# Two cross attentions in one kernel: where the weights of later stages are split into halves

## The reference

```
# layer 0: 8 heads of 16, no norm
Q = x @ W_q;  K, V = ctx @ W_k, ctx @ W_v
X = x + softmax(Q K^T / sqrt(16)) V @ W_o
x = X + relu(X @ w1.T + b1) @ w2.T + b2          # w1, w2: 512 x 512
# layer 1: 16 heads of 32, layernorm on both inputs
q = layernorm(x) @ Wq.T;  k, v = layernorm(ctx) @ Wkv.T
x = x + softmax(q k^T / sqrt(32)) v @ Wo.T + bo
out = x + silu(x @ W1.T + b1) @ W2.T + b2        # W1: 2048 x 512, W2: 512 x 2048
```

## Time and profile before

| | us |
|---|---|
| median of 3 runs | 5425.91 |
| lowest, highest | 5416.05, 5426.97 |
| the profiled execution | 5431.3 |
| its span on the core | 5429.5 |
| mean granted clock of TensorE | 0.975 of full speed |

### The profile page before, as it was taken

The page is one execution under the profiler, slowest core; times in us unless marked ns, Lnnn a source line. Parts: engine busy times, 40 slices in busy tenths (PEclk is TensorE's granted clock), DMA queues, the critical chain, the costliest instruction groups (busy, mean ns, idle before and its releaser), DMA issues. The chain is left out here.

```text
span 5429.5 us, 93007 instructions
## 1 busy us (share of the span) xinstructions
PE 5216.4 (96%) x27916; PEld 3335.3 (61%) x27916; DVE 4277.0 (79%) x6970; ACT 3251.5 (60%) x5920; POOL 2485.7 (46%) x1165
## 2 busy tenths in 40 slices
PE   8989999999799799999999999999999995999999
PEld 6844444444377566666666666666666662788887
DVE  6689999999577799999999999999999995432331
ACT  4258888888533377777777777777777773322222
POOL 0000000000000299999999999999999995000000
PEclk9989999999799799999999999999999997999999
DMA  7521111111344311111111111111111112332320
GB/s 218 130 51 36 38 39 39 38 37 32 93 124 128 107 33 45 46 45 46 37 41 45 46 45 45 32 46 45 46 45 33 45 33 86 117 97 87 100 93 24
DMA packets 340342, 341.18 MB, mean 63 GB/s; under 512 B 188304, under 2 KB 196368, under 8 KB 337936
## 3 DMA queue, kind: packets, MB, share of 16 engines
q1 hardware_dynamic: 339984, 336.71, 23.5%
HBM read 227.57 MB, written 108.92 MB: 62 GB/s over the span
## 5 line engine op out<-in xcount | busy, mean ns | idle before, releaser
L465 DVE TENSOR_REDUCE a_maxes<-a_mscore 128x1 f32<-128x458 f32 (+4 forms) x5376 | 3044.8, 626 | 218.6 <-PE a_mscore L526 163.1
L441 ACT ACTIVATE a_prob<-a_score 128x512 f32<-128x512 f32 x4992 | 2635.6, 602 | 891.8 <-PE a_score L535 855.9
L535 PE MATMUL a_score<-a_q,a_k 97*128 97x512 f32 (+1 forms) x4992 | 1937.1, 434 | 23.6 <-ACT a_prob L441 8.0
L526 PE MATMUL a_mscore<-a_k,a_qm 96*128 96x458 f32 (+4 forms) x5376 | 1837.8, 412 | 36.1 <-DMA a_k<-k 33.9
L410 POOL TENSOR_TENSOR a_added<-a_added,a_prob 128x1024 f32<-128x1024 f32 x640 | 1533.7, 2396 | 71.0
L526 PEld LDWEIGHTS a_mscore<-a_k,a_qm 96*128 96x128 f32 (+1 forms) x5376 | 1456.4, 309 | 131.2 <-DVE a_maxes L465 49.8
L535 PEld LDWEIGHTS a_score<-a_q,a_k 97*128 97x128 f32 (+1 forms) x4992 | 916.1, 193 | 974.4 <-ACT a_prob L441 587.1
L561 PE MATMUL a_acc<-a_prob,a_v 128*32 128x512 f32 x9984 | 1469.1, 604 | 1.1 <-ACT a_prob L441 0.7
L304 POOL MEMSET a_k<- 32x126 f32 (+4 forms) x6 | 6.3, 1053 | 1821.9 <-POOLq L60 1821.6
L556 PE MATMUL a_acc<-a_prob,a_ones 128*1 128x512 f32 x1280 | 611.6, 592 | 0.0
L482 DVE TENSOR_REDUCE a_vsum<-a_prob 128x256 f32<-128x768 f32 x512 | 528.5, 1033 | 31.6 <-POOL a_added L416 30.3
(11 more groups left out here) (208 smaller groups left out, 4063.3 us busy)
## 6 DMA issues: line engine op xcount, KB each, us to landing
e_part<-acc SPq DMA_DIRECT2D x120, 256.0 KB, 3.8
a_qm<-q SPq DMA_DIRECT2D x384, 64.0 KB, 1.9
a_q<-q SPq DMA_DIRECT2D x384, 64.0 KB, 1.9
acc<-a_acc_sb SPq DMA_DIRECT2D x384, 64.0 KB
a_k<-k SPq DMA_DIRECT2D x48, 416.0 KB, 6.6
q<-m_qout SPq DMA_DIRECT2D x128, 128.0 KB, 2.3
e_wo<-wo_split SPq DMA_DIRECT2D x32, 512.0 KB, 4.9
k<-kv_k1out SPq DMA_DIRECT2D x24, 512.0 KB, 2.9
```

Of the source, the lines that this page charges most:

```text
L441: act.activation(prob[:, t], score[SCORES[it.j][t]][:], ACT.Exp, scale=SCALE).then_inc(exp_done, 1)
L465: dve.tensor_reduce(maxes[j][:, t, c:c + 1], mscore[u % UNIT_BANKS][:, 0:wide], AX.X, ALU.max).then_inc(unit_read, 1)
L526: pe.matmul(mscore[u % UNIT_BANKS][:, 0:wide], qm[j][r:r + ROW, t:NB:NB // P], kt[kk][r:r + ROW, at:at + wide], start=True, stop=True).the ...
L535: pe.matmul(score[SCORES[it.j][t]][:], kt[it.k][r:r + C, i * P:(i + 1) * P], qt[it.j][r:r + C, :], start=True, stop=True).then_inc(score_d ...
```

## The change

The two layer-1 matrices that were split at the ends of the attentions, and three that were split in `middle` (`W_o`, `w1`, `w2`), are now split on GpSimd during a0. Eight jobs go through one staging tile `whole` and one pair `halves`: `W_o` (0.25 MB), `w1`, `w2`, `Wo`, and four row blocks of `W1` (1 MB each). SyncE loads job i at step i+1 and stores its halves to DRAM at step i+2. Steps are counted two a head: at the first item of a head, after `move_row` and ahead of `load_kv`, and at the sixth item of it. `middle` loads the halves of `W_o`, `w1` and `w2` where it loaded the whole matrices, twice the bytes, and splits `Wq` alone. a1 loads the eight half blocks of `W1` (1 MB each) at steps 1 to 8, and nothing in its opening. `ending` is unchanged.

```diff
--- before.py
+++ after.py
+        if splits:
+            whole = sb("whole", [P, KT * D], F32)
+            halves = [sb(f"half{i}", [P, KT * D], F32R) for i in range(2)]
+        KEPT = [16 * sum(2 * len(job[3]) for job in splits[:i]) for i in range(len(splits) + 1)]
...
+            def later_weights(step):
+                if 0 <= step - 2 < len(splits):
+                    job = splits[step - 2]
+                    sp.wait_ge(w_lo, step - 1)
+                    for i, half in enumerate(halves):
+                        for c, to in enumerate(job[3]):
+                            wide = job[2] // len(job[3])
+                            sp.dma_start(to[i], f32(piece(half, job)[:, :, c * wide:(c + 1) * wide])).then_inc(w_kept, 16)
+                if 0 <= step - 1 < len(splits):
+                    job = splits[step - 1]
+                    if step > 1:
+                        sp.wait_ge(w_lo, step - 1)
+                    sp.dma_start(piece(whole, job), job[0]).then_inc(w_loaded, 16)
+                if 0 <= step - 1 < len(loads):
+                    to, dram = loads[step - 1]
+                    sp.dma_start(f32(to), dram).then_inc(w_loaded, 16)
...
-            for dram, whole, _, _ in weights:
-                sp.dma_start(whole, dram).then_inc(w_loaded, 16)
             move_row(0, 0, 0)
...
+                if it.starts_head or (isinstance(it.qb, int) and it.qb == QB - 3):
+                    later_weights(it.h * 2 + (0 if it.starts_head else 1))
                 if it.starts_head and not it.first and not it.final_head:
                     load_kv(it.h + 1, 1 - it.k)
                 if it.last:
-                    for to, half in keep:
-                        sp.wait_ge(w_lo, len(weights))
-                        sp.dma_start(to, f32(half)).then_inc(w_kept, 16)
                     store(it.h, it.qb, it.j, it.n)
...
         def _(pool):
             fill(pool, 1)
+            for i, job in enumerate(splits):
+                pool.wait_ge(w_loaded, 16 * i + 16)
+                if i:
+                    pool.wait_ge(w_kept, KEPT[i])
+                hi, lo = (piece(half, job) for half in halves)
+                pool.tensor_copy(hi, piece(whole, job)).then_inc(w_hi, 1)
+                pool.wait_ge(w_hi, i + 1)
+                pool.tensor_tensor(lo, piece(whole, job), f32(hi), ALU.subtract).then_inc(w_lo, 1)
...
-                    if it.last and weights and t == SPLIT_AT:
-                        split_weights()
...
# middle
+            def load_halves(n, to):
+                for half, dram in zip(to, split[n]):
+                    sp.dma_start(f32(half[:]), dram).then_inc(w_loaded[n], 16)
...
-            load_weight("wo", staged["wo"][0], wo)
+            load_halves("wo", WO)
             load_acc(0)
-            load_weight("w1", staged["w1"][0], w1)
+            load_halves("w1", W1)
...
-            load_weight("w2", staged["w2"][0], w2)
+            load_halves("w2", W2)
...
-            split_weight("wo")
-            split_weight("w1")
             split_o(0)
-            split_weight("w2")
...
-            split_weight(0, "wo")
-            split_weight(1, "w1")
             normalise(0)
             split_o(0)
-            split_weight(2, "w2")
...
# build
+    first = {n: scratch(f"first_{n}", [2, P, kt, D]) for n, kt in (("wo", 1), ("w1", KT), ("w2", KT))}
+    w1_split = scratch("w1_later", [KT, 2, P, 1, F])
+    splits = [(tiles(a[f"L0_xattn_{n}"]), kt, D, [[first[m][i] for i in range(2)]])
+              for n, m, kt in (("W_o", "wo", 1), ("w1", "w1", KT), ("w2", "w2", KT))]
+    splits.append((tiles(a["L1_xattn_Wo"]), KT, D, [[wo_split[d, i] for i in range(2)] for d in range(KT)]))
+    splits += [(tiles(a["L1_xattn_W1"][r * P:(r + 1) * P, :]), 1, F, [[w1_split[r, i] for i in range(2)]])
+               for r in range(KT)]
+    attention(nc, "a0", *L0, q[0], k[0], v[0], row, acc[0], sums[0], splits)
...
+        attention(nc, "a1", *L1, q[1], k[1], v[1], row, acc[1], sums[1],
+                  loads=[(W1[i][:, r:r + 1, :], w1_split[r, i]) for r in range(KT) for i in range(2)])
```

More of the change, by code:

```diff
@@ L182, with attention @@
 VSUMS = len(ON_VECTOR) * PIECES
-def attention(nc, name, H, hd, q, k, v, row, acc_out, sums_out, weights=(), keep=()):
+def attention(nc, name, H, hd, q, k, v, row, acc_out, sums_out, splits=(), loads=()):
     SCALE = float(hd) ** -0.5
@@ L235, in attention, with piece @@
         acc_stored = [sem(f"acc_stored{i}") for i in range(2)]
+        if splits:
+            whole = sb("whole", [P, KT * D], F32)
+            halves = [sb(f"half{i}", [P, KT * D], F32R) for i in range(2)]
         w_loaded, w_hi, w_lo, w_kept = sem("w_loaded"), sem("w_hi"), sem("w_lo"), sem("w_kept")
+        KEPT = [16 * sum(2 * len(job[3]) for job in splits[:i]) for i in range(len(splits) + 1)]
+        def piece(tile, job):
+            return tile[:, 0:job[1] * job[2]].rearrange("p (k c) -> p k c", k=job[1])
         LOADS = 16 * 3 * HALVES
@@ L392, in _ @@
                 sp.wait_ge(side_stored, 16 * H * QB)
-            sp.wait_ge(w_kept, 16 * len(keep))
+            sp.wait_ge(w_kept, KEPT[-1])
+            sp.wait_ge(w_loaded, 16 * (len(splits) + len(loads)))
         @block.gpsimd
@@ L483, in add_up @@
                                   AX.X, ALU.add).then_inc(vsum_done, 1)
[L485 to L490, removed]
             fill(dve, 0)
@@ L513, in _ @@
                         add_up(it.n, it.first, *divmod(L.sum_at.index(t), PIECES))
-            if weights:
-                dve.wait_ge(w_lo, len(weights))
         @block.tensor
@@ L1521, in _, with middle @@
                 use_hidden(n, FT - 1)
-def middle(nc, name, acc, sums, recips, x, wo, w1, b1, w2, b2, gamma, beta, wq, x1, q):
+def middle(nc, name, acc, sums, recips, x, split, b1, b2, gamma, beta, wq, x1, q):
     H, BLOCKS, HT = sums.shape[1], T // NB, KT
@@ L1564, in middle @@
         early = [f32(qout[:, i:i + 2]).rearrange("p a b c -> p (a b) c") for i in (0, 2)]
-        staged = {"wo": (std[:].unsqueeze(1), WO), "w1": (y[:], W1), "w2": (early[0], W2)}
         gained_wq = early[1]
@@ L1643, in _ @@
         def _(act):
[L1644 to L1647, removed]
             def split_o(n):
@@ L1698, in _ @@
             act.wait_ge(const_loaded, 16 * 4)
-            act.wait_ge(w_lo, len(W_ORDER))
+            act.wait_ge(w_lo, 1)
             act.wait_ge(biasq_done, 1)
@@ L1720, in _ @@
         def _(dve):
[L1721 to L1724, removed]
             def normalise(n):
@@ L1813, in _ @@
                 dve.tensor_scalar(gained_wq[:, k], sq[:, k], gb[:, 0, k:k + 1], None, ALU.mult).then_inc(gained, 1)
[L1814 removed]
+            dve.wait_ge(w_hi, 1)
             dve.tensor_tensor(WQ[1][:], gained_wq, f32(WQ[0][:]), ALU.subtract).then_inc(w_lo, 1)
@@ L1870, in hidden @@
                 if n == 0:
-                    pe.wait_ge(w_lo, 2)
+                    pe.wait_ge(w_loaded["w1"], 32)
                 for m in range(HT):
@@ L1878, in project @@
                 if n == 0:
-                    pe.wait_ge(w_lo, 3)
+                    pe.wait_ge(w_loaded["w2"], 32)
                 for d in tiles:
@@ L1889, in queries @@
                 if n == 0:
-                    pe.wait_ge(w_lo, 4)
+                    pe.wait_ge(w_lo, 1)
                 for d in range(KT):
@@ L1900, in _ @@
             pe.wait_ge(consts_done, 2)
-            pe.wait_ge(w_lo, 1)
+            pe.wait_ge(w_loaded["wo"], 32)
             attended(0)
@@ L1958, in build @@
     wo_split = scratch("wo_split", [KT, 2, P, KT, P])
-    with ExitStack() as ctx:
[L1960 to L1971, removed]
-                      [(src, whole[:, i, :], W1[0][:, i, :], W1[1][:, i, :])
-                       for i, src in enumerate(rows(a["L1_xattn_W1"], a["L1_xattn_W1"].shape[1]))])
+    F = a["L1_xattn_W1"].shape[1]
@@ new lines, in build, with tiles @@
+    first = {n: scratch(f"first_{n}", [2, P, kt, D]) for n, kt in (("wo", 1), ("w1", KT), ("w2", KT))}
+    w1_split = scratch("w1_later", [KT, 2, P, 1, F])
+    def tiles(w):
+        return w.rearrange("(k p) c -> p k c", p=P)
+    splits = [(tiles(a[f"L0_xattn_{n}"]), kt, D, [[first[m][i] for i in range(2)]])
+              for n, m, kt in (("W_o", "wo", 1), ("w1", "w1", KT), ("w2", "w2", KT))]
+    splits.append((tiles(a["L1_xattn_Wo"]), KT, D, [[wo_split[d, i] for i in range(2)] for d in range(KT)]))
@@ new lines, in build @@
+    splits += [(tiles(a["L1_xattn_W1"][r * P:(r + 1) * P, :]), 1, F, [[w1_split[r, i] for i in range(2)]])
+               for r in range(KT)]
+    attention(nc, "a0", *L0, q[0], k[0], v[0], row, acc[0], sums[0], splits)
+    middle(nc, "m", acc[0], sums[0], recips[0], x, first, a["L0_xattn_b1"], a["L0_xattn_b2"], a["L1_xattn_ln_q_g"],
+           a["L1_xattn_ln_q_b"], a["L1_xattn_Wq"], x1, q[1])
+    with ExitStack() as ctx:
+        W1 = weight(nc, ctx, "w1", KT, F)
+        attention(nc, "a1", *L1, q[1], k[1], v[1], row, acc[1], sums[1],
```

(1 more changed line is left out.)

2 lines of the change are left out of this document (removed).

## The result

| | before | after |
|---|---|---|
| median of the runs timed side by side (7 and 7) | 5416.45 us | 5445.08 us |
| lowest, highest | 5413.88, 5426.97 | 5443.84, 5459.73 |
| ratio, 95% interval | | 1.0053 [1.0042, 1.0064] |
| the profiled execution, its span | 5431.3, 5429.5 | 5443.86, 5441.8 |

The change makes the kernel 28.6 us slower.

What follows compares the result with a forecast made beforehand. TensorE was taken to bound a0, TensorE and GpSimd both full in a1. Terms -10.1 - 1.2 + 2.7 + 24.8 = +16.2 us gave 5447.5 from the profiled 5431.3, 5442 on the median's scale; 8-in-10 range 5417 to 5450.

Steps and rivals of the forecast that it cites:

- step 1: End of a1: without VectorE's split beside GpSimd's adds, the last fold ends earlier, -10.1 us, bounds -8 to -11.5.
- step 2: End of a0: removing the split there gains nothing, and the eight stores end long before the final store, 0.
- step 3: Opening of a1: the first row store no longer stands behind 4 MB of W1, -1.2 us.
- step 4: Opening of middle: the reciprocals' store queues behind a doubled w1, +2.7 us, bounds -0.2 to +6.
- step 5: a0's second to fifth head starts: weights ahead of load_kv delay qm and stall TensorE, +24.8 us, bounds 0 to +32.
- Nothing makes it good: a0: the stalls of +24.8 us are not recovered, since TensorE is busy 98% of a0.
- The reasoning on SyncE: a0's head starts: SyncE can't hand over the value load until the weights drain, so query loads shift by the whole time.
- A: a0: SyncE is not held, only data queue; a0 costs 9, net +0.4, 5426; chance 0.22.
- B: a0: the DMAs hide; a0 costs 0 to 3, net -8.6 to -5.6, 5419; chance 0.12.
- C: B, with middle's store not held and a1 giving 11.5: -12.9, 5413; chance 0.10.
- D: a0 costs more, with stores at the slow rate, +7: net +23, 5449; chance 0.08.

Runs made afterwards that it cites:

- e0: The kernel before, unchanged, profiled a second time: 5422.12 us.
- e3: The kernel before plus eight 128 x 2048 splits on GpSimd in a0, with no DMA for them: 5417.95 us, ratio 1.0001.
- e7: The kernel before plus the change's weight loads and stores in a0 as DMAs alone, without GpSimd splits: 5462.22 us, ratio 1.0080.
- e9: The kernel before plus extra 1 MB stores at a0's head starts, 1 to 4 ahead of load_kv, then 3 and 4 behind: 5470.30 us, ratio 1.0098.
- e4: The kernel before with W1 alone split on GpSimd in a0 at sixth and eighth items and loaded as halves in a1: 5404.30 us, ratio 0.9979.
- e1: The changed kernel with the weight steps issued behind the next head's keys and values instead of ahead: 5433.20 us, ratio 1.0032 to the kernel before.
- e2: The changed kernel with steps at the sixth and eighth items, none at a head start: 5409.82 us, ratio 0.9987 to the kernel before.
- e5: e2 with the halves of w1 in middle loaded behind the reciprocals' store and load: 5403.88 us, ratio 0.9969 to the kernel before.
- e8: e5 with the job of Wo cut into two of half the columns: 5401.84 us, ratio 0.9972 to the kernel before.
- e6: e4 with middle's whole w1 loaded behind the store of the reciprocals: 5416.21 us, ratio 0.9982 to the kernel before.

## Why the prediction was right or wrong, step by step

The direction was right, the mechanism was right, and the size of the difference was not: +16.2 forecast, +28.6 measured. That 5442 came out near 5445.08 is luck, owed to a second error. The base, a median of three runs at 5425.91 and a profile at 5431.3, was high for this kernel: 5416.45 in the rounds of the result.

**The end of a1 (step 1): right.** Forecast -10.1, bounds -8 to -11.5. In the last two items the five adds take 12.45 and 12.43 us where the earlier trace rows had 15.91 for the item before the last. a1 as a whole took 2730.0 to 2733.2 in the five profiles with VectorE's split at its end (before, e0, e3, e7, e9), 2732.0 in the mean, and 2717.8 to 2723.9 in the seven without, 2720.9 in the mean: -11.1, with the opening's part (forecast together -11.3). e4 shows it without the rest of the change.

The reductions beside GpSimd's split in a0 are as they were. By shape (count, busy us, mean ns) this row stands in both stretches, 565.9 to 570.4 with GpSimd at work and 583.3 to 587.8 without:

```profile
L496 DVE TENSOR_REDUCE a_maxes<-a_mscore 128x1 f32<-128x418 f32 x3 | 1.8, 585 | 0.0
```

A job was estimated at 10 us of GpSimd; it is 6.5 (1.90 and 4.58). The `w_lo` wait never held SyncE: e7, which has none, has the same waits.

**The end of a0 (step 2): nothing, as said,** but the prediction didn't see what lay in that stretch of its profile: 11 us of low clock that other executions of the same kernel don't have. Had the time per matmul of the tail been read against the clock column, the base would have been questioned.

**The opening of a1 (step 3): right.** Forecast -1.2. From the first to the second `negmax` of a1 it takes 19.6 to 20.2 us in the five profiles with `W1` loaded in the opening and 18.2 to 19.2 in the seven without: -1.2 in the mean.

**The opening of middle (step 4): right.** Forecast +2.7. From the stage's start the normalise stands at 17.6 to 18.5 us in the six profiles with whole weights in the old order and at 20.4 to 20.8 in the three with halves, +2.4 in the mean (+2.9 forecast for this chain). The stage took 379.9 to 383.5 in these six (before, e0, e3, e4, e7, e9), 381.8 in the mean, and 383.0, 385.1 and 385.3 in those with halves (after, e1, e2): +2.7 in the mean, though the two groups overlap and a single pair of profiles (-0.2 here) can't show it. That the store queues behind `w1` was put to the test by e5.

**a0's head starts (step 5): the step that failed, in size.** It forecast stalls of 4.2, 6.8, 6.3 and 7.5 us, +24.8. The waits are at the forecast places and measure 5.13, 6.94, 7.44 and 8.21, 27.7 together, so the waits were 2.9 short. The sixth-item step of `Wo`'s eight stores, taken as 0 between 0 and 1, makes it wait 1.38; halving it (e8) takes that wait away. But the stage grew by 38.3. The five items are longer than the ordinary ones by 7.2, 9.9, 1.8, 9.8 and 10.7 us, 39.4 in all, that is 10.3 more than the 29.1 of the waits. This is the term that was missing: "Nothing makes it good" treated a stall as its own length, but behind the four long waits TensorE works at a clock of 0.50 for 4.0, 5.9, 4.7 and 5.1 us, and its first matmuls there take 0.92 us for two where they take 0.62 behind the short wait. At half speed that costs half the stretch, 2.0, 3.0, 2.4 and 2.5 us, and the four items are longer beyond their waits by 2.1, 3.0, 2.4 and 2.5. It is also the 9.5 us by which TensorE is busy longer. The wait of 1.38, behind which the clock held, cost 0.4 more.

The reasoning on SyncE held: query loads 9.15 us long, keys 5.17, no issue on time. Rivals A (SyncE is not held, a0 costs 9) and B and C (the DMAs hide) are out by these rows and by the 38 us, which e7 has without the splits. Rival D came nearest with its net +23, by stores at a slow rate, which would have made the waits 7 us longer; they are 2.9 longer, and the rest is the clock. What the prediction had wrong inside it is the share of the place: it blamed the position ahead of `load_kv`, and e1 shows that 27.5 of the 38.3 us in a0 stay when the weights go behind it, now because the data of `qm` queue, which is A's mechanism.

So the sum as the runs have it: -11.1 for a1, +2.7 for middle, +38.3 for a0, +29.9; measured 28.6.

## What to carry to other kernels

A stage whose engines idle and whose DMA share is 0.19 is still full at some places: lay added transfers against the tightest load of each item, and put them where no other bulk load stands (here a few items away: 35 us by the medians of the change and e2). Price a stall of the matmul engine as its length plus half of the stretch at half clock behind it, if the clock falls. And before a difference is built on one profile, compare stretches of equal work in it against its own clock column and against the spread of the runs.

## What the runs showed of the hardware that was not expected

- **A wait costs its length and half of the low clock behind it.** The six profiles of a0 with waits for `qm` of over 1 us (after, e1, e2, e5, e7, e9) have 23 of them. Behind 18 the clock fell, and TensorE worked 3.4 to 7.0 us at 0.50; the item is longer than the wait alone makes it by 1.8 to 3.3 us, which is half of that stretch to 0.2 us in each. Behind the other five (1.31 to 1.93 us) it held at 1.00, and the excess is 0.4. The length of the wait doesn't decide: the clock fell behind 1.54 us in e1 and held behind 1.93 in e2, and the excess is 3.1 behind 3.16 and 2.1 behind 10.42. The Trainium skill's page "TensorE: Matmul & The Clock Gate", section "What's actually happening", says that the clock is set by how busy the engine has been recently; the windows above agree, at 1.00 before the wait and 0.50 behind it.
- **The clock in a0's tail is one thing or the other.** It fell in the first profile of the kernel before, in e3 and in e6 (41 us), and held in the other nine (30.5 to 30.6 us), with the same 124 matmuls. All three have the split of `Wo` at a0's end, but so have four that held; and without that split three of e2's twelve runs are long too (5421.3 to 5427.3 at a mean clock of 0.975, the other nine at 0.978 to 0.980), though no profile shows where their clock fell. What decides it stays open.
- **Two engines at one port.** VectorE's split of `Wo` in a0's tail, with GpSimd idle, took 1.22 and 2.29 us. Beside GpSimd's adds have 1.51 and 4.36, and the three other pairs there took 2.28 to 3.40 and 4.31 to 4.34. The Trainium skill's page "SBUF — State Buffer", section "Who interferes with whom", says that a VectorE instruction with two SBUF inputs contends with GpSimd's reads, and of VectorE's two-port modes that one of the two engines has the shared port for its whole instruction while the other stands still. The trace agrees in size: the subtraction is longer by 2.0 to 2.1 us and the cast by 0.3 to 2.2, at most one of GpSimd's adds (2.39).

```profile
1402.76 1.22 DVE L488 CAST wo_hi<-wo_whole 128x2048 fp32r<-128x2048 f32 x1
...
1404.01 2.29 DVE L490 TENSOR_TENSOR wo_lo<-wo_whole,wo_hi 128x2048 fp32r<-128x2048 f32 x1
```
